# Last layer of a four-layer network: the scores and score maxima of the next sequence move among the experts of the current one

## The reference, cut to what matters

```python
# mixer: a state-space scan
u, z = split(xn @ in_proj.T); xs = silu(causal_conv(u) + b)       # 256 channels, 4 taps
dt, B, C = split(xs @ x_proj.T)                                   # 64, 16, 16
delta = softplus(softplus(dt @ dt_proj.T + dt_b) + dt_b)
state = exp(delta * A) * state + delta * xs * B                   # 16 states, scanned over time
s = ((sum over states of state * C) + xs * D) * silu(z) @ out_proj.T
# ffn: an attention block with a mixture of experts behind it
q, k, v = xn @ Wq + bq, xn @ Wk + bk, xn @ Wv + bv                # 16 heads of 8, q and k rotated
x1 = layernorm(xn + softmax(q k^T / sqrt(8)) v @ Wo + bo) * g1 + be1
comb = top 2 of softmax(x1 @ Wg + bg), normalised                 # 8 experts
y = sum_e comb_e * (gelu(x1 @ W1_e + b1_e) @ W2_e + b2_e)         # 128 -> 512 -> 128
ffn = layernorm(x1 + y) * g2 + be2
```

## Time and profile before

| | us |
|---|---|
| median of 3 runs (lowest, highest) | 3337.44 (3334.92, 3341.07) |
| the profiled execution | 3337.55 |
| its span in the profile | 3334.5 |
| PE / DVE / ACT busy over the span | 2837.0 / 2411.8 / 1673.1 |

### The profile page before, as it was taken

The page is one execution under the profiler, slowest core; times in us unless marked ns, Lnnn a source line. Parts: engine busy times, 40 slices in busy tenths (PEclk is TensorE's granted clock), DMA queues, the critical chain, the costliest instruction groups (busy, mean ns, idle before and its releaser), DMA issues. The chain is left out here.

```text
span 3334.5 us, 59646 instructions
## 1 busy us (share of the span) xinstructions
PE 2837.0 (85%) x19958; PEld 2305.0 (69%) x19958; DVE 2411.8 (72%) x6661; ACT 1673.1 (50%) x4013; POOL 321.0 (10%) x341
## 2 busy tenths in 40 slices
PE   2999999889999898989777288888888888888887
PEld 1887887778788787888667266666666666666665
DVE  2777777666666666666772378888888888888887
ACT  1333334355555555555443255556565655565554
POOL 0000000000000000000141411111111111111111
PEclk9999999999999999999889577777777777777777
DMA  6000000000000000000201133333333333333334
GB/s 195 0 0 0 0 0 0 0 1 0 0 0 0 0 0 0 0 0 0 71 16 53 46 106 95 89 89 87 90 88 96 84 95 90 96 83 91 95 96 108
DMA packets 86466, 163.18 MB, mean 49 GB/s; under 512 B 18856, under 2 KB 45616, under 8 KB 86320
## 3 DMA queue, kind: packets, MB, share of 16 engines
q0 software_dynamic: 20480, 62.93, 9.9%
q1 hardware_dynamic: 64640, 98.15, 9.2%
q10 hardware_dynamic: 1200, 0.27, 0.1%
HBM read 92.60 MB, written 9.99 MB: 31 GB/s over the span
## 5 line engine op out<-in xcount | busy, mean ns | idle before, releaser
L1034 ACT ACTIVATE b_neg<-b_neg,b_nmax 128x128 f32<-128x128 f32 (+1 forms) x512 | 228.4, 447 | 273.2 <-DVE b_nmax L1142 272.0
L2624 DVE TENSOR_TENSOR_SCAN d_state<-w,d_state 128x1024 f32<-128x1024 f32 x128 | 290.8, 2283 | 3.8 <-issue 3.4
L2361 ACT ACTIVATE d_probs<-l_bank,w_b 128x256 f32<-128x256 f32 x512 | 210.7, 469 | 155.7 <-PE l_bank L2199 153.3
L1130 DVE SCALAR_TENSOR_TENSOR b_gated<-b_th,l_bank 128x256 f32<-128x256 f32 x256 | 107.5, 420 | 208.2 <-ACT b_th L1028 203.9
L2199 PE MATMUL l_bank<-xnT,w_w 128*128 128x256 f32 x1024 | 245.1, 382 | 14.3 <-ACT d_probs L2361 14.3
L2210 PEld LDWEIGHTS l_bank<-w_w,d_probs 128*128 128x128 f32 x2048 | 244.9, 192 | 11.7 <-ACT d_probs L2361 5.3
L2210 PE MATMUL l_bank<-w_w,d_probs 128*128 128x128 f32 x2048 | 252.6, 276 | 0.0
L96 POOL TENSOR_TENSOR ln_rstd<-ln_var_eps,minus_half 128x2 f32<-128x2 f32 x51 | 64.6, 1267 | 1764.8 <-DVE ln_var_eps L90 1764.8
L2129 PE MATMUL l_bank<-w 9*128 9x256 f32 x1040 | 209.0, 669 | 25.0 <-ACT w L2284 18.9
L2323 ACT ACTIVATE w<-d_delta,d_negA 128x255 f32<-128x255 f32 x520 | 220.2, 499 | 0.0
L2199 PEld LDWEIGHTS l_bank<-xnT,w_w 128*128 128x128 f32 x1024 | 184.7, 190 | 40.9 <-ACT d_probs L2361 21.1
(11 more groups left out here) (404 smaller groups left out, 6814.4 us busy)
## 6 DMA issues: line engine op xcount, KB each, us to landing
d_bct<-l_bc SPq DMA_DIRECT2D x132, 512.0 KB, 3.9
d_state<-d_state POOLq DMA_DIRECT2D x96, 512.0 KB, 6.6
d_state<-d_state POOLq DMA_DIRECT2D x32, 256.0 KB, 3.8
x_sorted<-x SPq DMA_DIRECT2D x1, 2560.0 KB, 16.6
w<-in_L_ffn_w_dram SPq DMA_DIRECT2D x1, 2048.0 KB, 10.1
w_w<-in_L_ffn_W_dram SPq DMA_DIRECT2D x1, 2048.0 KB
c2e_xg<-x_sorted SPq DMA_DIRECT2D x16, 128.0 KB, 2.3
y_sorted<-c2e_yo SPq DMA_DIRECT2D x16, 128.0 KB, 1.8
```

Of the source, the lines that this page charges most:

```text
L1034: done = nc.scalar.activation(neg[:, h % RP, cols], neg[:, h % RP, cols], ACT.Exp, bias=nmax[:, h % RP, a:a + 1], scale=-1.0, accum_out=to ...
L2361: done = v.activation(hid[:, e % 2, k, :], bank[:, b, i * T:(i + 1) * T], ACT.Gelu, bias=w.b1[:, e, k:k + 1])
L2624: done = v.tensor_tensor_scan(group, dA[i][:, g % (NG - 1), :, :].rearrange("p m t -> p (m t)"), group, 0.0, ALU.mult, ALU.add)
```

## The change

- The banks are laid out anew: 0 to 3 (`four`) for all score blocks and `scoresT`, 4 and 5 for the hidden rows (`hid_bank`), 6 and 7 for the experts' outputs (`down_bank`). All four score blocks use the same banks, so each waits for the maxima of the one before it.
- On PE the q and k of n+1 are turned right after the attention of n (`turn_k` before the turn of y, `turn_q` after the output projection). The score blocks of n+1 stand behind `up(4)`, behind `up(6)`, behind `up(7)` and behind `down(6)`. The rows of b2 move behind `down(7)`.
- `AHEAD = 3`: three `scoresT` and exponentials instead of two are done before the loop's head.
- On DVE `take_qkv` and both `rotate` move into part 1, `times_c(1)` behind the division of the heads, `state_input(2)` behind the first inner norm, `first_part` behind expert 1, and the four `heads_max` among the experts.
- The residual is added by PE into the same PSUM bank (identity times `xn`, identity times `bo`), and POOL's `residual` goes. The inner norm is two passes (`inner_shift`, which needs no rstd, and `inner_scale`) instead of three. The router takes its best two from the exponentials without dividing by their sum.
- ACT copies k before the Silus, and q between the copy of x1T and `route_exp`.

```diff
+            def qkv_rows(m):
+                pe.wait_ge(xnT_ready, m + 1)
...
-                if blk >= 2:
-                    pe.wait_ge(max_ready, NBLK * n + blk - 1)
-                banks = back if blk % 2 else front
+                else:
+                    pe.wait_ge(max_ready, NBLK * m + blk)
...
-                    for k in range(2, HP):
+                    pe.wait_ge(b2_taken, n + 1)
+                    heads_out(0)
+                    for k in range(AHEAD, HP):
                         scoresT(n, k)
-                        if k % 2 == 0:
-                            heads_out(k // 2 - 1)
-                        if k == 5:
+                        if k == 4:
+                            heads_out(1)
                             turn_x(n + 1, 1 - par)
+                        if k == 6:
+                            heads_out(2)
+                            qkv_rows(n + 1)
...
-                    pe.wait_ge(xnT_ready, n + 2)
-                    qkv_rows(0)
+                    turn_k(n + 1)
                     pe.wait_ge(y_ready, n + 1)
...
+                    pe.wait_ge(v_taken, n + 2)
+                    nc.tensor.matmul(attended, c.ident[:, :], xn[:, par, :, :], start=True, stop=False)
+                    nc.tensor.matmul(attended, c.ident[:, :], wide_bo, start=False, stop=False)
                     pe.wait_ge(yT_ready, n + 1)
...
+                    turn_q()
                     project_uz()
-                    qkv_rows(1)
...
-                        if e == 4:
+                        if e == 2:
+                            scores(n + 1, 0)
+                        if e == 3:
                             pe.wait_ge(comb_ready, n + 1)
...
+                        if 4 <= e <= 6:
+                            scores(n + 1, e - 3)
...
-                    attention_front(n + 1)
+                    turn_q_less_max(n + 1)
+                    for p in range(AHEAD):
+                        scoresT(n + 1, p)
                     out_rows(n)
...
+            def inner_shift(out, src, weight):
+                for a in range(TILES):
+                    v.scalar_tensor_tensor(out=out[:, a, :], in0=src[:, a, :], scalar=meanvar[:, a, 0:1],
+                                           in1=weight[:, :], op0=ALU.subtract, op1=ALU.mult)
...
+            def inner_scale(out, bias, count):
+                v.drain()
                 dve.wait_ge(rstd_ready, count)
...
+                    done = v.scalar_tensor_tensor(out=out[:, a, :], in0=out[:, a, :], scalar=rstd[:, a:a + 1],
+                                                  in1=bias[:, :], op0=ALU.mult, op1=ALU.add)
...
                     add_expert(0)
                     scan(2, 1)
+                    add_expert(1)
+                    first_part(n + 1)
+                    add_expert(2)
                     times_c(2)
-                    add_expert(1)
+                    heads_max(n + 1, 0)
+                    add_expert(3)
                     scan(3, 0)
-                    add_expert(2)
+                    add_expert(4)
                     scan(3, 1)
+                    heads_max(n + 1, 1)
+                    add_expert(5)
                     times_c(3)
-                    add_expert(3)
-                    take_qkv(n + 1, 1)
-                    rotate(0)
-                    add_expert(4)
-                    rotate(1)
-                    v.drain()
-                    add_expert(5)
-                    first_part(n + 1)
+                    heads_max(n + 1, 2)
                     add_expert(6)
+                    heads_max(n + 1, 3)
                     add_expert(7)
```

More of the change, by code:

```diff
@@ L1909, in layer3 @@
         bank = ctx.enter_context(nc.psum_tensor("l3_bank", [P, 8, 512], F32))
-        front, back = bank[:, 4:8, :], bank[:, 0:4, :]
+        four, hid_bank, down_bank = bank[:, 0:4, :], bank[:, 4:6, :], bank[:, 6:8, :]
         KF = F3 // P
@@ L2100, in turn_heads, with turn_k, turn_q, scores @@
                 return done
[L2102 to L2111 removed]
+            def turn_k(m):
+                pe.wait_ge(rot_ready, m + 1)
+                turn_heads(1, down_bank).then_inc(kT_in_psum, 1)
+            def turn_q():
+                turn_heads(0, four[:, 0:2, :]).then_inc(qT_in_psum, 1)
+            def scores(m, blk):
+                if blk == 0:
+                    pe.wait_ge(qT_ready, 2 * m + 1)
+                    pe.wait_ge(kT_ready, m + 1)
+                    pe.wait_ge(dt_taken, m + 1)
+                else:
+                    pe.wait_ge(max_ready, NBLK * m + blk)
+                if blk == 1 and later(m):
+                    pe.wait_ge(combT_ready, m)
                 for a in range(TILES):
@@ L2114, in scores @@
                         own = slice(ROWS * g, ROWS * g + HD3)
-                        done = nc.tensor.matmul(banks[:, g, a * T:(a + 1) * T], qT[own, blk, a * P:(a + 1) * P],
+                        done = nc.tensor.matmul(four[:, g, a * T:(a + 1) * T], qT[own, blk, a * P:(a + 1) * P],
                                                 kT[own, blk, :], start=True, stop=True,
@@ L2168, in _ @@
             pe.wait_ge(xnT_ready, 1)
-            for a in range(TILES):
-                qkv_rows(a)
+            qkv_rows(0)
             project_uz()
@@ L2173, in _ @@
             project_dt(0)
-            attention_front(0)
+            turn_k(0)
+            turn_q()
+            for blk in range(NBLK):
+                scores(0, blk)
+            turn_q_less_max(0)
+            for p in range(AHEAD):
+                scoresT(0, p)
             with pe.Fori(0, NSEQ // 4) as m:
@@ L2344, in _ @@
             copy_xdbl(0)
+            copy_k(0)
+            copy_q(0)
             log_part(0, 0)
-            copy_qk(0)
             log_part(0, 1)
             copy_qm(0)
-            for p in range(2):
+            for p in range(AHEAD):
                 exp_scores(0, p)
+            for i in range(CI):
+                decays(0, 0, i)
             with act.Fori(0, NSEQ // 4) as m:
@@ L2360, in gelu @@
                                 k = 2 * b + i
-                                done = v.activation(hid[:, e % 2, k, :], bank[:, b, i * T:(i + 1) * T], ACT.Gelu,
+                                done = v.activation(hid[:, e % 2, k, :], hid_bank[:, b, i * T:(i + 1) * T], ACT.Gelu,
                                                     bias=w.b1[:, e, k:k + 1])
                             done.then_inc(hid_ready, 1)
-                    for p in range(2, HP):
+                    for p in range(AHEAD, HP):
                         exp_scores(n, p)
-                        if p == 6:
+                        decays(n, (p - 1) // 2, (p - 1) % 2)
+                        if p == 4:
                             copy_xnT(n + 1)
@@ L2519, in take_qkv, with take_v @@
                 dve.wait_ge(qkv_in_psum, TILES * m + a + 1)
-                v.tensor_tensor(qkv[:, a, :], bank[:, 6 + a, 0:2 * D], bq, ALU.add)
-                v.tensor_tensor(vaug[:, a, :, 0:HD3], bank[:, 6 + a, 2 * D:3 * D].rearrange("p (h v) -> p h v", v=HD3),
-                                bv, ALU.add).then_inc(qkv_taken, 1)
+                v.tensor_tensor(qkv[:, a, :], bank[:, 4 + a, 0:2 * D], bq, ALU.add)
+            def take_v():
+                for a in range(TILES):
+                    done = v.tensor_tensor(vaug[:, a, :, 0:HD3],
+                                           bank[:, 4 + a, 2 * D:3 * D].rearrange("p (h v) -> p h v", v=HD3), bv, ALU.add)
+                done.then_inc(v_taken, 1)
             def rotate(a):
@@ L2607, in _ @@
                 v.drain()
+            take_v()
             first_part(0)
@@ L2653, in _ @@
                     scan(1, 1)
-                    times_c(1)
+                    for a in range(TILES):
+                        take_qkv(n + 1, a)
+                    for a in range(TILES):
+                        rotate(a)
+                    v.drain()
                     dve.wait_ge(o_turned, n + 1)
```

181 lines of the change are left out of this document (81 added, 100 removed).

## The result

The changed kernel took 3365.16 us (median of 4 runs, 3362.59 to 3371.28), the kernel before 3336.61 beside it: a ratio of 1.0091, interval 1.0078 to 1.0103. The forecast was 3328, faster; the measured time lies inside the stated range of 3290 to 3382, on the other side of the kernel before. The profiled execution took 3371.28 with a span of 3369.6, some 6 us above the median.

A forecast was written before the change was run, and what follows sets the result against it. DVE nearly sets the pace, with PE as busy. Front +2.6, experts +5.4, tail -8.9 give -0.9 a sequence, -15 in all; +2 for the first sequence and +3 for the clock make -10 on 3337.55: 3328 us, range 3290 to 3382.

The forecast's parts named there:

- The clock: At `down(7)` behind score block 3: a fall costs 1.3 us in two or three of 16 sequences, 3 us added.
- four signs of being wrong: Score blocks of 2 us, `down(7)` at 1.2 GHz, DVE waiting over 2 us in the tail, first stage not longer.
- The experts: From `down(0)` to the end of expert 7: 33.1 us instead of 27.7, 5.4 later, by DVE's longer list.
- The tail: After expert 7: 16.1 us instead of 25.0, 8.9 less, with the maxima gone from DVE there.
- The front: Up to `down(0)`: 35.8 us instead of 33.2, 2.6 later, through ACT's queue before the first Gelu.
- The start of the layer: First sequence: three hand-overs cost 4 to 6 us once, attention starts 3.5 earlier: +2 (between -3 and +6).
- Rival 2: Front: residual products, `turn_k`, `turn_q`, part of u at 1.2 GHz; +2 us a sequence, 3360; chance 0.16.
- Rival 1: Score block 3 and `down(7)`: bad hand-over, clock low in each sequence; +4 us a sequence, 3392; chance 0.17.
- Rival 4: Front: earlier full-size work raises the clock sooner, `down(0)` 1.5 to 2 us earlier; 3300; chance 0.10.
- the 2.4 us of DVE work: DVE work saved a sequence: router 0.7, residual add 0.5, norms 1.2; not all gained, because waits move.

The follow-up runs named there:

- e15_best: The changed kernel with `copy_q` and `first_part` later, score block 0 earlier, and added unread full-size PE products, four of them ahead of `turn_x`: 3322.62 us.
- e1_tail: The changed kernel with score blocks and maxima put back behind the experts, in two sets of banks: 3418.90 us.
- e13_tail2: The changed kernel with scores and maxima back in the tail, as e1_tail, but third `scoresT` and its exponential behind `out_rows`, Tanh ahead of the exponentials: 3358.75 us.
- e4_last: The changed kernel with score block 3 behind `down(7)` and the last maxima behind expert 7: 3377.04 us.
- e14_resid: The changed kernel with the residual formed by POOL and added by DVE again, without the two residual products on PE: 3398.20 us.
- the two reorderings: The changed kernel with `copy_q` behind the Gelu of expert 1, and `first_part` behind `times_c(2)` with score block 0 ahead of `up(4)`: 3351.96 us.
- e9_warmer: The changed kernel with ten added full-size PE products a sequence that nobody reads: 3334.62 us.
- e5_warm: The changed kernel with 7 added full-size PE products a sequence that nobody reads: 3343.77 us.
- e6_norms: The kernel before with only the two-pass inner norms and the router without its division: 3326.98 us.

## Why the prediction was wrong

**The clock, the step that failed.** The prediction saw the place: "Where the clock falls there, `down(7)` ends 1.8 later and expert 7 1.3 later", and then "I count 1.3 in two or three sequences of 16", 3 us in all. The runs show it in 12 of 16. The low clock costs elsewhere too. In the tail it falls again, while PE waits for ACT and DVE, and stays low into the next front. The forecast had walked that front at the low clock up to the heads, at t = 19.3; they came at 19.0 to 20.9, 19.8 on average, against the 18.2 of most sequences of e15_best. The two falls are separate: e1_tail, e13_tail2, e4_last and e14_resid kept `down(7)` at the high clock in 15 or 16 sequences and have fronts of 36.7 to 38.4. The forecast's loop was 12 us shorter than before (-15 and +3), the measured one 31.7 longer: 44 us apart. With ten more products a sequence and no other edit 30.5 us of them are gone; with e15's products on top of the two reorderings 29.3 (3351.96 to 3322.62). So this term was of the order of 30 us, ten times its size. The stages agree: of the 3.1 us a sequence that the changed kernel lies above the forecast 0.7 are longer score blocks (below), and in e9_warmer, with the clock kept up, 2.7 are gone: 0.9 in the front, 0.6 in the experts, 1.1 in the tail. The figure is what the added products recover; in the front that is a little more than the forecast had missed. e5_warm has 21 of the 30 us although its `down(7)` still falls in 11 sequences, so that the place that the prediction watched is the smaller part. How often the clock falls could not be read from the trace before, where the order is another. The prediction did price all 16 sequences at the low level, +64 us, but as a rival with a chance of 0.17, and put 3 us into the sum. Of its four signs of being wrong two came: `down(7)` ran partly at 1.2 GHz, and DVE waited up to 2.8 us in the tail (L2572 above).

The prediction weighed a rule here: the Trainium skill ("TensorE: Matmul & The Clock Gate", Part 1) has the low clock as the default, released by activity, and by that the score blocks could have kept the clock up. The trace after is against that use of the rule: in 12 sequences the clock fell right behind a wait of 1.3 to 1.5 us and a score block, within `down(7)`. That more work on PE goes with a higher clock the windows of e5_warm and e9_warmer do show, 0.88 and 0.91 instead of 0.79.

**The experts.** Forecast 33.1; 33.87 where the clock holds (e9_warmer). The hand-over went as walked, but a little later from maxima 0 on. DVE's timeline, after, of the sequence from 2563.45, with `down(0)` at 2598.95; it answers to the earlier trace rows:

```profile
2583.14 0.37 DVE L2684 RECIPROCAL d_recip<-l_bank 128x16 f32<-128x16 f32 x2 [1.58 <-PE l_bank L2236]
...
2600.94 0.61 DVE L2664 SCALAR_TENSOR_TENSOR same_head<-l_bank,d_comb,d_x 128x128 f32<-128x128 f32 x2 [1.58 <-PE l_bank L2217]
...
2607.24 0.87 DVE L2563 TENSOR_SCALAR d_dv<-l_bank,w_dt_b 128x256 f32<-128x256 f32 x2 [2.18 <-PE l_bank L2093]
...
2612.86 2.29 DVE L2614 TENSOR_REDUCE d_qk<-l_bank 128x8 f32<-128x2048 f32 x1 [0.57 <-issue]
...
2630.03 2.29 DVE L2614 TENSOR_REDUCE d_qk<-l_bank 128x8 f32<-128x2048 f32 x1 [0.49 <-PE l_bank L2125]
2632.48 0.61 DVE L2664 SCALAR_TENSOR_TENSOR same_head<-l_bank,d_comb,same_head 128x128 f32<-128x128 f32 x2 [0.16 <-issue]
...
2638.70 0.61 DVE L2608 SCALAR_TENSOR_TENSOR same_head<-same_head,d_rstd,w_be 128x128 f32<-128x128 f32 x2 [1.37 <-POOL d_rstd L2431]
2639.56 0.69 DVE L2572 SCALAR_TENSOR_TENSOR d_delta<-d_dv,d_dneg 128x512 f32<-128x512 f32 x1 [0.24 <-ACT d_dneg L2337]
```

Dt came at D = 8.3 (8.25), maxima 0 end at 16.2 (15.5), block 3 is seen at 31.1 (30.2), expert 7 ends at 34.1 (33.1). The 0.7 a sequence, 11 us in all, come to a good part from score blocks of 1.15 us; both bounds, 1.0 and 2.05, had been named, and 1.0 was a little low. The other 0.6 of the experts' 34.50 is the clock.

**The tail.** The steps held: rstd 5.7 us after expert 7 (5.6), the third part at 6.6 (6.2), the end at 16.4 (16.1) in a sequence of this kind. What was missing is again the clock: 16.6 to 16.8 in most sequences and 18.67 in three; with the added products of e9_warmer they took 15.7 to 16.2.

**The front.** +3.3 instead of +2.6. ACT's queue was as foretold; its rows, after, beside the earlier trace rows:

```profile
2592.09 1.03 ACT L2307 ACTIVATE w<-l_bank 128x1024 f32<-128x1024 f32 x1
2593.14 1.28 ACT L180 ACT_TABLE_LOAD   x1
2594.70 0.22 ACT L180 ACTIVATE d_r_logits<-d_r_logits 128x16 f32<-128x16 f32 x1 [0.28 <-DVE d_r_logits L173]
2594.94 1.28 ACT L2381 ACT_TABLE_LOAD   x1
2596.23 1.57 ACT L2381 ACTIVATE d_probs<-l_bank,w_b 128x256 f32<-128x256 f32 x4
```

The copy of q, the table load, the exponential and the second load stand in that order, and `down(0)` starts 2.7 us after the Gelu. The heads decide the rest: at t = 18.2 the front is 34.0 (e5_warm), at 20.9 it is 37.6. My 35.8 lies between the two, and close to the mean of 36.4. The working has two small slips here: by its own terms PE is done with the projection at 19.3 + 1.9 + 0.4 + 0.9 + 0.7 = 23.2, not 23.0, and ACT's chain starts from 22.8. (In the sum, 16 x 0.9 is 14.4, not 15.) Together they are worth some 6 us, towards the time that was measured.

**The start of the layer.** +8.4 up to the loop, where +2 had been forecast for the start and the first sequence together: three hand-overs between maxima and score blocks of 2.21 us each (forecast 4 to 6 together), and 2.6 more for the second logarithm. In the first sequence DVE then waits 3.59 instead of 0.38 for the first decays; ACT now has a third exponential ahead of them. Its front is 1.7 longer than before, 1.6 less than the others grew, so that the whole is near +7 and beyond the range of -3 to +6 given. The hand-overs are borne out by e1_tail: with two sets of banks the waits of 2.21 are gone, and the stretch takes 42.1. The layer's own beginning, which the change does not touch, moves by up to 7 us between the profiled executions of these kernels (1886.5 to 1893.4).

**The rivals.** Rival 2's time, 3360, is nearest, but by luck: it has the front 2 us a sequence longer than the forecast, and it was 0.7 longer. Its mechanism is half right: `turn_k` and the residual products do run at 1.2 GHz in most sequences, `turn_q` (1.04) and u (3.62) do not, and without the residual products the front is longer (e14_resid). Rival 1 has the place right (block 3, `down(7)`) and the size wrong: the clock mostly falls for a short while and costs 0.6 in the experts, and with the tail 1.8 a sequence beside e9_warmer, where +4 was given; by its own mark of 0.9 it counts as having come. Rival 4 has the direction of the clock wrong. Of the 2.4 us of DVE work saved in a sequence, the 1.9 of the norm and the router were worth 0.5 where they were tried by themselves (e6_norms).

What stays open: why the fall at `down(7)` comes in 12 of 16 sequences, in a cycle of four (a turn of the loop has four sequences); how the 30 us divide exactly between the two falls; and whether another order, without products that nobody reads, would keep the clock as well.

## What to carry to other kernels

Where TensorE's granted clock is below 1.00 in some stage of a loop, a new order of its work has a term that no sum of durations at one clock shows, and it can lie in a stage that had 1.00 before, as `down(7)` did here. Write it with the price of every sequence at the low level as its bound. Ask what PE runs and what it waits for ahead of each chain, and compare the same instruction's duration in several sequences of the trace. Work taken from a nearly full engine pays only for the part that is not waiting on the others after the change; test small savings by themselves (here 0.3%) before they are joined to a large reordering (here 0.9% slower, of which they are a part).

## What was not expected of the hardware

- Products that nobody reads, placed where PE waits, made the changed kernel 21 to 30 us faster and raised the granted clock of the loop from 0.79 to 0.88 and 0.91. Seven such products a sequence cost the kernel before 17 us, and 25 with the smaller norms, though its clock rose as well.
- Taking two products off PE made what PE ran next slower: in e14_resid the turn of q took 1.91 us instead of 1.04 and u 4.5 instead of 3.62, at a lower clock.
- The clock can fall within one group of equal products and be high again in the next: 16 products of `down(7)` took 2.05 us in four sequences and 3.1 to 3.6 in twelve, and the turn of q behind them took 1.09 to 1.10 in nine of the twelve.
- Within one execution the changed kernel's sequences differ by up to 3.9 us (85.8 to 89.7) with the same instructions in them, those of the kernel before by 1.6.
